# Last stage of a six-layer decoder: residuals and biases moved into TensorE's products, norms read from PSUM and ended on ScalarE

## The chip, the cores and the metric

The kernel runs on one core of one Trainium2 chip. The metric is the device time of one execution in microseconds. The kernel before takes 3324.82 us, the median of three runs (3321.77 to 3327.7).

## The reference, cut to what matters

Six residual layers follow one another, each ended by a layer norm without weights. The change touches the last stage of the kernel, which computes the last two layers on B = 2 sequences of S = 2048 tokens and D = 512 channels, all in float32:

```
x = layernorm(x + xattn(x, ctx))      # 16 heads of 32, 8 context rows per head (stride 16)
x = layernorm(x + tree(x))

xattn: Q = x Wq^T + bq; K, V from ctx with bk, bv
       out = softmax(Q K^T / sqrt(32)) V, then  @ Wo^T + bo
tree:  q = x Wq^T; gate = sigmoid(q routers^T)        # 255 inner nodes
       leaf_prob = product of the branch gates, depth 8 -> 256 leaves
       out = (leaf_prob @ leaf_values) @ Wout^T + Wout_b
layernorm(x) = (x - mean) / sqrt(var + 1e-5)
```

## The kernel before, in words

`decoder` calls five stages one after the other; a barrier lies between them. The last is `strided_attention_and_tree` (line 2361). It first loads all weights and multiplies them together once (`multiply_weights`, line 2503): the keys with Wq into `qk`, with the query bias as a row `qk_bias`; the values with Wo into `vo`; Wq of the tree with the routers into `wr`; the leaf values with Wout into `lo`. ScalarE copies each product out of PSUM (`keep_products`, line 2622).

Then it works through 16 tiles of 128 tokens of both sequences (b = 0 and 1). The work on one tile is spread over six steps of a software pipeline: step n handles tile n in its first part and tiles n-1 to n-5 in later ones. Each engine has its own `step(n)` (TensorE line 2598, ScalarE 2633, VectorE 2739, GpSimd 2483, the DMA queue SP 2458), executes it in the written order, and waits on counting semaphores. `pipelined` (line 44) writes the first six steps out, loops over pairs of steps, and writes the last ones out. Buffers with two places are chosen by `n.parity`.

The path of one tile, with the buffers that a later tile waits for:

- step n: `scores` (one-row product of the bias, four products with `xT`, for each b) into bank 0; VectorE `shift` (maximum per head, subtraction); ScalarE exp; VectorE `soften` (sum, reciprocal, product) into `probs`.
- step n+1: TensorE turns the probabilities (`turn_probabilities`, bank 1), ScalarE copies them, `attend` multiplies with `vo` into banks 2 and 3. VectorE `sum_attention` adds `x_bo`, which GpSimd has made of x and the bias; then statistics and aggregates (lines 168, 173), GpSimd's root of two operations (lines 189, 191), and `finish_attention` (line 184 by way of `Norm.finish`) writes `mid`.
- step n+2: `turn_mid` turns `mid` into bank 6, half by half (b), ScalarE copies each half (line 2646), `gates` multiplies with `wr` into bank 7, ScalarE tanh (line 2654) and an affine step (line 2657) make `gate`.
- step n+3: VectorE `walk_tree`, 16 dependent operations over 1 to 256 columns, two of them a level. GpSimd adds the output bias to `mid` into `mid_wb` (line 2490).
- step n+4: `turn_leaves` turns the leaf probabilities into bank 6, ScalarE copies them (line 2641), `feed` multiplies with `lo` into banks 4 and 5.
- step n+5: VectorE `sum_tree` adds `mid_wb`, statistics, GpSimd's root, `finish_tree` writes `o`; the next step stores it.

Bank 6 serves both `turn_mid` and `turn_leaves`. VectorE's step places the other operations between those of the tree by the index i of `walk_tree`; `soften` and `finish_attention` come behind it. TensorE's order in a step is: probabilities(n-1), leaves(n-4), scores(n), feed(n-4), mid(n-2) first half, attend(n-1), mid second half, gates(n-2) for both halves. With `Norm`, y is a tensor in SBUF, and PSUM is free again once VectorE has added; the sum's wait is in `sum_attention` and `sum_tree`.

Of the kernel before, what the change touches and what calls it, by code (L numbers as in the profile page):

```python
# [12 lines left out]
P = 128  # L13
F32 = mybir.dt.float32
BF16 = mybir.dt.bfloat16
ALU = mybir.AluOpType
# [9 lines left out]
class Tile:  # L26
# [8 lines left out]

    def slot(self):

        return slice(self.index, self.index + 1) if isinstance(self.index, int) else bass.ds(self.index, 1)
# [5 lines left out]
def pipelined(eng, steps, lag, step, more=1):  # L44

    first = lag + more + (steps - lag - more) % 2
    for n in range(first):
        step(Tile(n, n % 2, steps, n))  # L50
    with eng.Fori(0, (steps - first) // 2) as pair:
        step(Tile(pair * 2 + first, first % 2, steps, first))
        step(Tile(pair * 2 + (first + 1), (first + 1) % 2, steps, first + 1))
    for n in range(steps, steps + lag):
        step(Tile(n, n % 2, steps, n))
# [73 lines left out]
class Norm:  # L129
# [5 lines left out]
    def __init__(self, m, name, rows, summed=None):  # L135
        self.rows, self.summed = rows, summed
        self.y = m.sbuf(f"{name}_y", [P, rows, D])
# [49 lines left out]
    def root(self, pool, n, eps, exponent):  # L187
# [3 lines left out]
        pool.tensor_tensor(self.rstd[:], self.var_eps[:], exponent[:, 0:self.rows], ALU.pow).then_inc(self.rooted, 1)  # L191

# [1648 lines left out]


class ScaledNorm(Norm):


    def __init__(self, m, name, rows, summed=None):
        super().__init__(m, name, rows, summed)
        self.shift = m.sbuf(f"{name}_shift", [P, rows])
        self.finished = m.sem(f"{name}_finished")
        self.OPS = self.SUMMED + 2 * rows  # L1850
        self.ROOT_OPS = 4

    def root(self, pool, n, eps, exponent, zero):
        wait(pool, self.done, n, self.OPS, self.MOMENTS)
        wait(pool, self.finished, n, self.rows, 0)
        mean = self.moments[:, :, 0]
        pool.tensor_tensor(self.var_eps[:], self.moments[:, :, 1], eps[:, 0:self.rows], ALU.add).then_inc(self.rooted, 1)
        wait(pool, self.rooted, n, self.ROOT_OPS, 1)
        pool.tensor_tensor(self.rstd[:], self.var_eps[:], exponent[:, 0:self.rows], ALU.pow).then_inc(self.rooted, 1)
        wait(pool, self.rooted, n, self.ROOT_OPS, 2)  # L1860
        pool.tensor_tensor(self.shift[:], mean, self.rstd[:], ALU.mult).then_inc(self.rooted, 1)
        wait(pool, self.rooted, n, self.ROOT_OPS, 3)
        pool.tensor_tensor(self.shift[:], zero[:, 0:self.rows], self.shift[:], ALU.subtract).then_inc(self.rooted, 1)

    def finish(self, act, n, r, target):
        wait(act, self.rooted, n, self.ROOT_OPS, self.ROOT_OPS)
        act.activation(target, self.y[:, r], ACT.Identity, bias=self.shift[:, r:r + 1], scale=self.rstd[:, r:r + 1]).then_inc(self.finished, 1)

# [492 lines left out]
def strided_attention_and_tree(nc, x_in, xT_in, ctxT, weights, consts, out):  # L2361
# [8 lines left out]
    with ExitStack() as ctx:  # L2370
# [7 lines left out]
        bo_rep = sb("bo_rep", [P, D])  # L2378
        wb_rep = sb("wb_rep", [P, D])
# [6 lines left out]
        banks = [ps(f"bank{i}", [P, 512]) for i in range(8)]  # L2386
# [12 lines left out]
        CTX_LOADS, ATTENTION_LOADS, TREE_LOADS = 5, 3, 6  # L2399
# [4 lines left out]
        xb_sb = sb("x_bo", [P, 2, B, D])  # L2404
# [8 lines left out]
        mid = sb("mid", [P, 2, B, D])  # L2413
        midb = sb("mid_wb", [P, 2, B, D])
# [7 lines left out]
        norm_a, norm_f = Norm(m, "norm_a", B), Norm(m, "norm_f", B)  # L2422
# [4 lines left out]
        xb_done, midb_done = sem("xb_done"), sem("midb_done")  # L2427
# [6 lines left out]
        b_s, b_pT, b_o, b_f, b_T, b_g = banks[0], banks[1], banks[2:4], banks[4:6], banks[6], banks[7]  # L2434
# [4 lines left out]
        with nc.Block() as block:  # L2439
            @block.sync  # L2440
            def _(sp):
# [10 lines left out]
                sp.dma_start(ident[:], consts["ident"]).then_inc(attention_here, 16)  # L2452
                for to, k in ((mats["fq"], "fq"), (routersT, "routersT"), (leafT, "leafT"), (mats["outT"], "outT")):
                    sp.dma_start(to[:], block_rows(w[k])).then_inc(tree_here, 16)
                sp.dma_start(bo_rep[:], w["bo"].partition_broadcast(P)).then_inc(tree_here, 16)
                sp.dma_start(wb_rep[:], w["wb"].partition_broadcast(P)).then_inc(tree_here, 16)

                def step(n):
# [4 lines left out]
                    if t := n.back(LAG + 1):  # L2463
                        wait(sp, norm_f.done, t, norm_f.OPS, norm_f.OPS)
                        sp.dma_start(out_view[bass.ds(t.index * P, P)], o_sb[:, t.parity]).then_inc(stored[t.parity], 16)
                    if n:
                        wait(sp, xb_done, n, B, -B)
# [7 lines left out]
            def _(pool):  # L2475
                pool.memset(half[:], -0.5)
                pool.memset(eps[:], LN_EPS)
                pool.memset(center[:], 0.5).then_inc(ready, 1)
                pool.memset(ones[:], 1.0).then_inc(ready, 1)
                pool.memset(ones_row[:], 1.0).then_inc(ready, 1)  # L2480
                pool.wait_ge(tree_here, 16 * TREE_LOADS)

                def step(n):
                    if t := n.back(5):
                        norm_f.root(pool, t, eps, half)
                    if t := n.back(3):
                        wait(pool, norm_a.done, t, norm_a.OPS, norm_a.OPS)
                        wait(pool, norm_f.done, t, norm_f.OPS, norm_f.SUMMED - 2 * norm_f.OPS)
                        for b in range(B):
                            pool.tensor_tensor(midb[:, t.parity, b], mid[:, t.parity, b], wb_rep[:], ALU.add).then_inc(midb_done, 1)  # L2490
                    if n:
                        here(pool, x_here, n, 16)
# [352 lines left out]
```

## Time and profile before

| | |
|---|---|
| median of three runs | 3324.82 us |
| the profiled execution | 3335.67 us |
| its span, first to last instruction | 3333.9 us |
| mean granted TensorE clock | 0.894 |
| busy over the span: TensorE / VectorE / ScalarE / GpSimd | 81% / 75% / 35% / 19% |
| busy from 2975 to the end (359 us): TensorE / VectorE / ScalarE / GpSimd | 297.5 / 244.7 / 66.8 / 111.9 us |
| granted clock in that part | 0.86 |

The stages follow one another in time, so shares over the whole span say little of one of them. In the rows below, times are microseconds from the start of the span. PE is TensorE, DVE VectorE, ACT ScalarE, POOL GpSimd; L2564 is line 2564 of the kernel. A float32 product of 512 columns shows as two MATMUL rows, a transpose of 128 columns as one. Matmuls overlap each other in the rows, so what one costs is read from the distance between starts.

### The profile page before, as it was taken

What the parts mean: (1) busy time and instruction counts of PE and PEld (TensorE: products, weight loads), DVE (VectorE), ACT (ScalarE), POOL (GpSimd) and SP (SyncE); (2) the same over time, 40 slices, a digit from 0 to 9 for tenths busy, and PEclk for the clock granted to TensorE, in tenths of its full rate; (3) what the DMA queues carried; (4) which work ended last, traced back from release to release, by engine and by line L of the source; (5) the groups of instructions that cost most, each with busy time, mean ns of one, the idle gap of its engine ahead of it and who ended that gap; (6) DMA issues with size and microseconds to landing.
All of it is one profiled execution on the core that took longest, in us unless ns stands there. A gap on an engine that the chain in (4) does not pass through costs nothing. (4 is left out here: it accounts for less than half of the span.)

```text
span 3333.9 us, 88364 instructions
## 1 busy us (share of the span) xinstructions
PE 2692.8 (81%) x35334; PEld 1912.9 (57%) x35356; DVE 2510.2 (75%) x4464; ACT 1182.5 (35%) x2016; POOL 620.9 (19%) x800
## 2 busy tenths in 40 slices
PE   7577777777777755999999995697769999968987
PEld 5455655555555543677777763344456767646664
DVE  6888887888888872477777783887857787834887
ACT  5233333333333320122222221654446565521221
POOL 3232222333322221000000000002600000002343
PEclk9789888888888866999999997899989999988888
DMA  3000000010000101301111112545941212142231
GB/s 88 3 15 28 29 28 29 28 29 28 29 28 29 47 22 64 128 20 51 51 50 50 50 48 89 196 176 179 319 116 51 76 50 76 59 143 83 83 94 51
DMA packets 229643, 234.68 MB, mean 70 GB/s; under 512 B 24112, under 2 KB 157872, under 8 KB 229296
## 3 DMA queue, kind: packets, MB, share of 16 engines
q1 hardware_dynamic: 229296, 229.70, 21.6%
q8 instruction: 261, 4.28, 0.5%
q14 instruction: 86, 0.70, 0.1%
HBM read 136.84 MB, written 92.81 MB: 69 GB/s over the span
## 5 line engine op out<-in xcount | busy, mean ns | idle before, releaser
L1132 PE MATMUL ctxatt_banks<-ctxatt_xT,ctxatt_wq 128*128 128x256 f32 x1024 | 232.9, 381 | 2.9 <-ACT ctxatt_qT L1208 2.1
L1171 PE MATMUL ctxatt_banks<-ctxatt_wo,ctxatt_oT 128*128 128x512 f32 x512 | 230.8, 604 | 4.9 <-DVE ctxatt_norm_y L1277 4.9
L826 DVE TENSOR_TENSOR delta_a<-delta_t_sys 128x30 f32<-128x30 f32 (+14 forms) x480 | 223.3, 465 | 10.3
L849 DVE SCALAR_TENSOR_TENSOR delta_conv<-delta_line,delta_conv_w,delta_conv 128x256 f32<-128x256 f32 x384 | 206.9, 560 | 3.4 <-DVE delta_ss L772 2.1
L829 DVE TENSOR_TENSOR delta_t_sys<-delta_t_sys,delta_a 128x30 f32<-128x30 f32 (+14 forms) x480 | 200.2, 417 | 11.4
L1132 PEld LDWEIGHTS ctxatt_banks<-ctxatt_xT,ctxatt_wq 128*128 128x128 f32 x1024 | 190.0, 191 | 28.7 <-ACT ctxatt_qT L1208 3.3
L393 POOL TENSOR_TENSOR delta_conv<-delta_conv,delta_product 128x256 f32<-128x256 f32 x192 | 148.7, 784 | 263.0 <-ACT delta_product L658 262.7
L508 PE MATMUL delta_banks<-delta_states,delta_kqT 32*32 32x32 f32 x4096 | 60.3, 209 | 154.0 <-DVE delta_states L868 95.2
L489 PE MATMUL delta_banks<-delta_xT,delta_wkT 128*128 128x256 f32 x512 | 135.9, 416 | 43.3 <-ACT delta_beta_T L640 35.8
L656 ACT ACTIVATE delta_conv<-delta_line,delta_conv_b,delta_conv_w 128x256 f32<-128x256 f32 x192 | 115.3, 601 | 153.3 <-POOL delta_conv L393 141.6
L1171 PEld LDWEIGHTS ctxatt_banks<-ctxatt_wo,ctxatt_oT 128*128 128x128 f32 x512 | 96.4, 193 | 117.0 <-issue 110.5
L668 ACT ACTIVATE delta_u<-delta_banks 128x256 f32<-128x256 f32 x64 | 23.9, 373 | 385.6 <-PE delta_banks L508 385.6
L2080 PE MATMUL wkv_banks<-wkv_woT,wkv_oT 128*128 128x512 f32 x256 | 131.6, 673 | 36.0 <-DVE wkv_oT L2278 36.0
L489 PE MATMUL delta_banks<-delta_xT,delta_wqT 128*128 128x256 f32 x512 | 151.8, 450 | 0.0
L489 PE MATMUL delta_banks<-delta_xT,delta_wvT 128*128 128x256 f32 x512 | 143.9, 432 | 3.8 <-ACT delta_line L646 3.8
L508 PEld LDWEIGHTS delta_banks<-delta_states,delta_kqT 32*32 32x32 f32 x4096 | 52.5, 121 | 161.1 <-issue 161.0
L1218 ACT ACTIVATE ctxatt_probsT<-ctxatt_banks 128x512 f32<-128x512 f32 x128 | 69.4, 594 | 204.7 <-PE ctxatt_banks L1153 204.7
L2070 PE MATMUL wkv_banks<-wkv_mixed,wkv_wkT 128*128 128x256 f32 x512 | 118.0, 384 | 29.5 <-DMA wkv_wrT<-L_attn_wrT 29.5
L489 PEld LDWEIGHTS delta_banks<-delta_xT,delta_wkT 128*128 128x128 f32 x512 | 102.2, 206 | 64.6 <-issue 23.7
L499 PE MATMUL delta_banks<-delta_kqT 32*32 32x64 f32 x4096 | 91.3, 250 | 57.0 <-DVE delta_kqT L795 28.6
L189 POOL TENSOR_TENSOR ctxatt_norm_var_eps<-ctxatt_norm_moments,ctxatt_eps 128x2 f32<-128x2 f32 x16 | 3.1, 194 | 714.3 <-DVE ctxatt_norm_moments L173 714.3
L1271 DVE COPY ctxatt_oT<-ctxatt_banks 128x512 f32<-128x512 f32 x64 | 44.1, 690 | 119.3 <-PE ctxatt_banks L1163 119.3
(328 smaller groups left out, 6728.3 us busy)
## 6 DMA issues: line engine op xcount, KB each, us to landing
h<-ffn_hid SPq DMA_DIRECT2D x66, 256.0 KB, 2.0
ffn_hid<-h SPq DMA_DIRECT2D x6, 1536.0 KB, 13.0
wkv_xT<-xT SPq DMA_DIRECT2D x64, 129.0 KB, 2.8
delta_xT<-xT SPq DMA_DIRECT2D x64, 128.0 KB, 3.0
delta_x<-x SPq DMA_DIRECT2D x16, 512.0 KB, 3.6
xT<-delta_newT SPq DMA_DIRECT2D x64, 128.0 KB, 2.8
x<-delta_new SPq DMA_DIRECT2D x16, 512.0 KB, 3.5
ctxatt_xT<-xT SPq DMA_DIRECT2D x64, 128.0 KB, 2.6
```

The costliest lines, as they stand in the source:

```text
L393: pool.tensor_tensor(conv[:, i, g], conv[:, i, g], product[:, p % PRODUCTS], ALU.add).then_inc(tap_added, 1)
L489: mm = pe.matmul(b_proj[:, p % 2, 0:B * P], wT[NAMES[i]][:, k, g * P:(g + 1) * P], xT_sb[:, n.parity, k], start=k == 0, stop=k == KB - 1)
L499: mm = pe.matmul(cols[h, j], kqT[h, n.parity, 0, g * QI + j], kqT[h, n.parity, :, g * QI + j], start=True, stop=True)
L508: mm = pe.matmul(cols[h, lane], lhsT(h, lane), right(h, lane), start=True, stop=True)
L656: act.activation(conv[:, i, g].rearrange("p (b t) -> p b t", b=B), ln[:, :, 0:P], ACT.Identity, bias=conv_b[:, i, g:g + 1], scale=conv_w[: ...
L826: c.did(dve.tensor_tensor(terms, t_sys[:, j + 1:, j:j + 1].to_broadcast([P, rows, j]), t_sys[:, j:j + 1, 0:j].to_broadcast([P, rows, j]), ...
L829: c.did(dve.tensor_tensor(to, to, terms, ALU.add))
L849: c.did(dve.scalar_tensor_tensor(to, line[:, i, g, :, j:j + P], conv_w[:, i, g, j:j + 1], to, ALU.mult, ALU.add))
L1132: mm = pe.matmul(b_q[:, i * B * P:(i + 1) * B * P], wq[:, k, pair * P:(pair + 1) * P], xT_sb[:, n.parity, k], start=k == 0, stop=k == KB - 1)
L1171: mm = pe.matmul(b_o[:], oT[:, b, k, :], wo[:, k, :], start=k == 0, stop=k == PAIRS - 1)
L2070: mm = pe.matmul(bank(i, q)[:, j * WCOLS:(j + 1) * WCOLS], mats[name][:, k, u * P:(u + 1) * P], mixed[:, n.parity, i, k].rearrange("p b t ...
L2080: mm = pe.matmul(banks[:, OUT_BANK + r], oT[:, n.parity, k, r * P:(r + 1) * P], mats["woT"][:, k], start=k == 0, stop=k == KB - 1)
```

## The change

Both residual additions move to TensorE: a product with the identity matrix writes x (or the middle result) into the PSUM bank, and the product with the weights adds to it. The biases are added to `vo` (a sixteenth of it per head, since each head's probabilities sum to one) and to `lo` by a one-row product while the weights are multiplied. The norms read their input from PSUM, and the normalisation is an activation with scale and shift on ScalarE (`ScaledNorm`, which the stage before already used; its root has four operations on GpSimd in place of two). `x_bo`, `mid_wb` and GpSimd's additions are gone. `mid` has four places, chosen by `n.quarter`, and the loops of four engines are written over four steps (`pipelined_by_four`). The order within the steps of TensorE, ScalarE and VectorE is a new one. The DMA queue waits for `norm_f.finished` (ScalarE) and for `attended` (TensorE), and loads the biases as single rows.

```diff
@@ weights' products
-jobs.append((D, [(kv[1][:, e, b, :], mats["woT"][:, e, :]) for e in range(KB)]))
+jobs.append((D, [(kv[1][:, e, b, :], mats["woT"][:, e, :]) for e in range(KB)] + [(share_row[:], bo_row[:])]))
...
-jobs.append((D, [(leafT[:, e, l * P:(l + 1) * P], mats["outT"][:, e, :]) for e in range(KB)]))
+jobs.append((D, [(leafT[:, e, l * P:(l + 1) * P], mats["outT"][:, e, :]) for e in range(KB)] + [(ones_row[:], wb_row[:])]))
@@ TensorE
+                def start_attention(n):
+                    here(pe, x_here, n, 16)
+                    for b in range(B):
+                        wait(pe, norm_a.finished, n, B, b + 1 - B)
+                        pe.matmul(b_o[:, b], ident[:], x_sb[:, n.parity, b], start=True, stop=False)
 def attend(n):
     wait(pe, pT_kept, n, 1, 1)
     for b in range(B):
-        wait(pe, norm_a.done, n, norm_a.OPS, b + 1 - norm_a.OPS)
-        pe.matmul(b_o[b][:], pT_sb[...], vo[:, b, :], start=True, stop=True).then_inc(attended, 1)
+        pe.matmul(b_o[:, b], pT_sb[...], vo[:, b, :], start=False, stop=True).then_inc(attended, 1)
+                def start_tree(n):
+                    for b in range(B):
+                        wait(pe, norm_f.finished, n, B, b + 1 - B)
+                        pe.matmul(b_f[:, b], ident[:], mid[:, n.quarter, b], start=True, stop=False)
 def step(n):
-    turn_probabilities(t1); turn_leaves(t4, t3); scores(n); feed(t4)
-    turn_mid(t2, 0); attend(t1); turn_mid(t2, 1); gates(t2, 0); gates(t2, 1)
+    scores(n); start_attention(t1); turn_probabilities(t1)
+    start_tree(t4); turn_leaves(t4, t3); turn_mid(t2, 0); attend(t1)
+    turn_mid(t2, 1); gates(t2, 0); feed(t4); gates(t2, 1)
@@ ScalarE
+                def finish_attention(n, b):
+                    wait(act, midT_made, n, B, -B)
+                    wait(act, fed, n, B, -3 * B)
+                    norm_a.finish(act, n, b, mid[:, n.quarter, b])
+                def finish_tree(n, b):
+                    gone(act, stored, n, 16)
+                    norm_f.finish(act, n, b, o_sb[:, n.parity, b])
 def step(n):
-    probsT(t1); leafpT(t4); midT(t2, 0); midT(t2, 1); exps(n); gate_leaves(t2)
+    finish_tree(t5, 0); finish_tree(t5, 1); probsT(t1); leafpT(t4); midT(t2, 0)
+    exps(n); midT(t2, 1); gate_leaves(t2); finish_attention(t1, 0); finish_attention(t1, 1)
@@ VectorE, in the loop over the 16 tree operations i
-    walk_tree; sum_tree at 0, 1; norm_f.statistics at 2, 3; norm_f.aggregate at 4, 5; shift at 6, 7
-    finish_tree at 8, 9; sum_attention at 10, 11; norm_a.statistics at 12, 13; aggregate at 14, 15
-    behind the loop: soften(n); finish_attention(t1)
+    norm_f.statistics at 0, 1 and norm_f.aggregate at 2, 3, each ahead of walk_tree; shift at 4, 5
+    soften(n) at 11; norm_a.statistics at 12, 13; norm_a.aggregate at 14, 15
@@ GpSimd
-    norm_f.root(t5); mid_wb(t3); x_bo(n); norm_a.root(t1)
+    norm_f.root(t5); norm_a.root(t1)
```

The step functions are shown as the list of their calls; each part runs where its tile exists.

## Rows read from the trace of the kernel before

**Rows 1.** Timeline: start, duration in us, engine, line; [idle before <-releaser]
```profile
3032.24 0.48 PE L2555 MATMUL tree_bank<-tree_qk_bias,tree_ones_row 1*128 1x128 f32 x2 [0.69 <-ACT tree_lo L2630]
...
3094.40 0.60 ACT L2654 ACTIVATE tree_th<-tree_bank 128x512 f32<-128x512 f32 x1 [2.56 <-PE tree_bank L2564]
...
3191.90 0.60 ACT L2654 ACTIVATE tree_th<-tree_bank 128x512 f32<-128x512 f32 x1 [2.56 <-PE tree_bank L2564]
...
3226.30 0.60 ACT L2654 ACTIVATE tree_th<-tree_bank 128x512 f32<-128x512 f32 x1 [2.56 <-PE tree_bank L2564]
...
3260.90 0.60 ACT L2654 ACTIVATE tree_th<-tree_bank 128x512 f32<-128x512 f32 x1 [2.56 <-PE tree_bank L2564]
...
3276.82 0.60 ACT L2654 ACTIVATE tree_th<-tree_bank 128x512 f32<-128x512 f32 x1 [2.56 <-PE tree_bank L2564]
...
3328.97 1.00 DVE L184 TENSOR_SCALAR tree_o<-tree_norm_f_y,tree_norm_f_moments,tree_norm_f_rstd 128x512 f32<-128x512 f32 x2 [1.16 <-POOL tree_norm_f_rstd L191]
```

**Rows 2.** Timeline, TensorE's products of one step at full clock
```profile
3162.48 0.44 PE L2572 MATMUL tree_bank<-tree_ident,tree_probs 128*128 128x128 f32 x2 [0.59 <-DVE tree_probs L2699]
...
3162.75 0.60 PE L2587 MATMUL tree_bank<-tree_ident,tree_leaf 128*128 128x128 f32 x4
...
3163.28 0.48 PE L2555 MATMUL tree_bank<-tree_qk_bias,tree_ones_row 1*128 1x128 f32 x2
...
3166.19 3.60 PE L2595 MATMUL tree_bank<-tree_lo,tree_leafpT 128*128 128x512 f32 x8
...
3169.62 0.60 PE L2547 MATMUL tree_bank<-tree_ident,tree_mid 128*128 128x128 f32 x4
...
3170.06 1.88 PE L2579 MATMUL tree_bank<-tree_vo,tree_probsT 128*128 128x512 f32 x4
...
3172.22 3.62 PE L2564 MATMUL tree_bank<-tree_wr,tree_midT 128*128 128x256 f32 x16
```

**Rows 3.** VectorE by line: durations ns min/median/max; then groups, busy us, mean ns
```profile
L184 DVE TENSOR_SCALAR tree_o<-tree_norm_f_y,tree_norm_f_moments,tree_norm_f_rstd x32: 533/1406/1540, 3100.1 to 3329.4; 128x512 f32<-128x512 f32 x32
...
L2733 DVE TENSOR_TENSOR tree_norm_f_y<-tree_bank,tree_mid_wb 128x512 f32<-128x512 f32 x32 | 21.7, 686 | 3.0 <-PE tree_bank L2595 2.5
...
L168 DVE BATCH_NORM_STATS2 tree_norm_f_stats<-tree_norm_f_y 128x6 f32<-128x512 f32 x32 | 21.5, 686 | 0.0
```

**Rows 4.** Waits from 3099 to 3284: us in total, times, longest
```profile
PE tree_bank L2572 <- DVE tree_probs L2699: 19.8, 11, 2.9
```

**Rows 5.** Windows: us, PE, PEld, DVE, ACT, POOL busy, PEclk, DMA share, GB/s
```profile
3162.00:3164.00 2.00, 1.52 (x10) 1.24 (x11) 1.82 (x5) 1.89 (x4) 0.33 (x1) 1.00 0.00 0
...
3192.00:3194.00 2.00, 0.00 (x0) 0.00 (x0) 1.93 (x8) 1.22 (x2) 0.90 (x2) 1.00 1.01 321
...
3196.00:3198.00 2.00, 2.00 (x10) 1.77 (x9) 2.00 (x8) 0.04 (x1) 0.00 (x0) 0.50 0.00 0
```

**Rows 6.** Timeline, two groups of transposes into bank 6 with the copy between
```profile
3301.15 0.60 PE L2547 MATMUL tree_bank<-tree_ident,tree_mid 128*128 128x128 f32 x4
...
3302.50 0.66 PE L2547 MATMUL tree_bank<-tree_ident,tree_mid 128*128 128x128 f32 x4 [0.75 <-ACT tree_midT L2646]
```

**Rows 7.** Timeline, from the gates' products to the first tree operation
```profile
3289.90 3.62 PE L2564 MATMUL tree_bank<-tree_wr,tree_midT 128*128 128x256 f32 x16
...
3295.05 0.16 DVE L2727 TENSOR_TENSOR tree_paths<-tree_ones,tree_gate 128x2 f32<-128x2 f32 x1
```

**Rows 8.** Timeline, root and normalisation of ScaledNorm in the stage before
```profile
2963.70 0.20 POOL L1857 TENSOR_TENSOR wkv_norm_var_eps<-wkv_norm_moments,wkv_eps 128x2 f32<-128x2 f32 x1 [16.08 <-DVE wkv_norm_moments L173]
...
2965.36 1.52 ACT L1867 ACTIVATE wkv_new<-wkv_norm_y,wkv_norm_shift,wkv_norm_rstd 128x512 f32<-128x512 f32 x2 [2.98 <-POOL wkv_norm_shift L1863]
```

**Rows 9.** ScalarE by line: durations ns min/median/max
```profile
L2646 ACT ACTIVATE tree_midT<-tree_bank x32: 597/597/599, 3058.4 to 3303.2; 128x512 f32<-128x512 f32 x32
...
L2657 ACT ACTIVATE tree_gate<-tree_th,tree_center x16: 721/722/724, 3066.2 to 3307.3; 128x512 f32<-128x512 f32 x16
```

**Rows 10.** Timeline, the last feed of the drain
```profile
3319.32 6.14 PE L2595 MATMUL tree_bank<-tree_lo,tree_leafpT 128*128 128x512 f32 x8 [0.69 <-ACT tree_leafpT L2641]
```

More of the change, by code:

```diff
@@ L53, in pipelined, with pipelined_by_four @@
         step(Tile(pair * 2 + (first + 1), (first + 1) % 2, steps, first + 1))
+    for n in range(steps, steps + lag):
+        step(Tile(n, n % 2, steps, n))
+def pipelined_by_four(eng, steps, lag, step, more=1):
+    first = lag + more + (steps - lag - more) % 4
+    for n in range(first):
+        step(Tile(n, n % 2, steps, n))
+    with eng.Fori(0, (steps - first) // 4) as four:
+        for k in range(4):
+            step(Tile(four * 4 + (first + k), (first + k) % 2, steps, first + k))
     for n in range(steps, steps + lag):
@@ L1839, in _ @@
                     pipelined(pe, FSTEPS, 3, step)
[L1843 to L1867, printed above, removed]
 WT = P
@@ L2385, in strided_attention_and_tree @@
         ones_row = sb("ones_row", [1, P])
-        banks = [ps(f"bank{i}", [P, 512]) for i in range(8)]
+        share_row = sb("share_row", [1, P])
+        zero = sb("zero", [P, B])
+        all_banks = ps("banks", [P, 8, 512])
+        banks = [all_banks[:, i] for i in range(8)]
         mats = {k: sb(k, [P, KB, D]) for k in ("wkT", "wvT", "wq", "woT", "fq", "outT")}
@@ L2477, in _ @@
                 pool.memset(eps[:], LN_EPS)
+                pool.memset(zero[:], 0.0)
                 pool.memset(center[:], 0.5).then_inc(ready, 1)
                 pool.memset(ones[:], 1.0).then_inc(ready, 1)
-                pool.memset(ones_row[:], 1.0).then_inc(ready, 1)
-                pool.wait_ge(tree_here, 16 * TREE_LOADS)
+                pool.memset(ones_row[:], 1.0)
+                pool.memset(share_row[:], 1.0 / XH).then_inc(ready, 1)
                 def step(n):
                     if t := n.back(5):
[L2485 to L2492, printed above, removed]
-                        wait(pool, norm_a.done, n, norm_a.OPS, norm_a.SUMMED - 2 * norm_a.OPS)
-                        for b in range(B):
-                            pool.tensor_tensor(xb_sb[:, n.parity, b], x_sb[:, n.parity, b], bo_rep[:], ALU.add).then_inc(xb_done, 1)
+                        norm_f.root(pool, t, eps, half, zero)
                     if t := n.back(1):
-                        norm_a.root(pool, t, eps, half)
-                pipelined(pool, STEPS, LAG, step)
+                        norm_a.root(pool, t, eps, half, zero)
+                pipelined_by_four(pool, STEPS, LAG, step)
             @block.tensor
@@ new lines, in gate_leaves @@
+                def gate_leaves(n):
+                    wait(act, gated, n, B, B)
+                    wait(act, gate_done, n, 1, 0)
+                    act.activation(th[:], b_g[:], ACT.Tanh, scale=0.5).then_inc(th_done, 1)
+                    wait(act, th_done, n, 1, 1)
+                    wait(act, tree, n, TREE_OPS, 0)
+                    act.activation(gate[:].rearrange("p b n -> p (b n)"), th[:], ACT.Identity, bias=center[:], scale=0.5).then_inc(gate_done, 1)
+                def finish_attention(n, b):
+                    wait(act, midT_made, n, B, -B)
+                    wait(act, fed, n, B, -3 * B)
+                    norm_a.finish(act, n, b, mid[:, n.quarter, b])
@@ L2760, in step @@
                             norm_a.aggregate(dve, t1, b)
-                    if n:
-                        soften(n)
-                    for b in range(B):
-                        if t1:
-                            finish_attention(t1, b)
                 keep_keys_and_values()
-                pipelined(dve, STEPS, LAG, step)
+                pipelined_by_four(dve, STEPS, LAG, step)
 def decoder(nc, a, out):
```

173 lines of the change are left out of this document (93 added, 80 removed).

## The prediction

> **What bounds the kernel now.** The page gives 3333.9 us to this execution; the last stage begins near 2975 and all edits lie in it. Read first the timeline of ScalarE's tanh (line 2654), whose input is the last product of a step: it marks the end of each step. Step 4 ends at 3094.40 and step 15 at 3276.82, so the middle takes 182.4 / 11 = 16.58 us a step. Ahead lie 62.2 us from the first scores at 3032.24, behind it 57.1 us to the end of the span [rows 1].
>
> Next, TensorE's own rows of one step at full clock [rows 2]: probabilities turned 0.27, leaves turned 0.53, scores 2.91, feed 3.43 (four products of 512 columns, 0.86 each), half a middle result turned 0.44, attend 1.72 (two products), the other half 0.44, gates 3.44: 13.18 us, with 0.18 of drain behind. VectorE is the longer engine in such a step: one normalisation into tree_o takes 1.41 us by its median and 0.53 at its least, and each sum out of PSUM 0.69 [rows 3]. TensorE waits for VectorE's probabilities, 19.8 us in 11 waits [rows 4]. Where it waited over 2 us, its granted clock stood at 1.00 (2.4 GHz) in the gap and at 0.50 (1.2 GHz) 2 us behind it; where it was idle for 0.5 of 2 us, the clock stayed at 1.00 [rows 5]. The step from 3260.90 to 3276.82, 15.9 us, is one at full clock and VectorE's; the pair of steps that ends at 3226.30 holds a fall and took 34.4 [rows 1], 2.6 more than two such. So both engines are near the bound, VectorE at full clock and TensorE behind a fall.
>
> **VectorE and GpSimd: removed.** Per step four sums (4 x 0.69), the normalisations into tree_o (2 x 1.41) and those into tree_mid leave VectorE, over 6 us [rows 3]. GpSimd's four additions of 128x512 go with them. I price that at nothing in the middle: with over 6 us out of 15.9, VectorE is no longer last, and what is late next is TensorE.
>
> **TensorE: added.** Four identity products of 512 columns a step, two for x and two for the middle result. They have the form of the feed's products, so 4 x 0.86 = 3.44 us at full clock [rows 2]. The low bound is the rate of this kernel's transposes, four of 128 columns in 0.44 us, or 4 x 0.44 = 1.76. I take 3.44, since these are ordinary products. TensorE then has 16.62 us of work a step. In the weights' products four one-row products of 512 columns are added, all on an unbroken run: +3.4 us, low bound 1.8.
>
> **A wait inside the step.** The leaves are turned into bank 6 and, in the new order, the first half of the middle result follows directly into the same bank; before, scores and feed lay between. So TensorE waits for ScalarE's copy. The same pattern stands at the end of the trace: from one group of four transposes to the next, with the copy between, 1.35 us [rows 6]. In place of the 0.53 of rows 2 that is +0.82. This wait is sure.
>
> **A wait at the step's start.** PSUM banks now hold y until ScalarE has normalised it, and start_tree wants banks 4 and 5 in the same step in which the norm is read. Let T be the end of the gates. The first tree operation starts at T+1.53 [rows 7], and the second half's statistics are queued behind it on VectorE: they start at T+1.63, and the two aggregates among three tree operations end at T+2.8. GpSimd's root now has four operations; the stage before runs the same four, and from its first to ScalarE's start are 1.66 us [rows 8]. So ScalarE normalises from T+4.5. It took 0.76 a half there from SBUF. For PSUM I take off 0.125, the distance between a 128x512 activation out of SBUF (0.722) and out of PSUM (0.597) [rows 9], which gives 0.64; bounds 0.60 and 0.81. The first bank is free at T+5.2, the second at T+5.85. TensorE, after scores 2.91, identity products for x 1.72 and probabilities 0.27, is there at T+4.7 and waits 0.5 us. Queued behind it: leaves, middle, attend, gates, feed; on ScalarE the copies behind the normalisation. From T+5.21: 1.72 + 1.35 + 0.44 + 1.72 + 0.44 + 1.72 + 3.43 + 1.72 + 0.18 = 12.72, so the step takes **17.93 us**, 1.35 more than now. Bounds: 17.44 without this wait, 18.5 with root and activations at their longest.
>
> The Trainium skill, "VectorE: DVE Perf Modes", section on the TRN2 errata, gives VectorE 62 cycles of 0.96 GHz more for a PSUM source than for SBUF and ScalarE 52 cycles of 1.2 GHz less, 0.065 and 0.043 us. In the trace the sum out of PSUM (0.686) and the statistics out of SBUF (0.686) show no such step [rows 3], and ScalarE's distance is 0.125. By the page an estimate of the step would be 18.08, and the whole 1.6 us longer.
>
> **Other edits.** Scores come ahead of the probabilities; covered, since scores need only VectorE's shift. soften moves up to the eleventh tree operation, waits there for exps, which ScalarE does behind the first middle copy (T+10), and ends at T+11.4; the probabilities are wanted 11 us later. norm_a ends at T+14.4 on VectorE and 1.7 us later on GpSimd, ahead of ScalarE's turn at T'+1.4; its banks are free at T'+2.1 and T'+2.7 under scores of 2.91. If that cover went, it would cost up to 1.5 a step. SP's store waits for finish_tree (T+6.5) and so moves the next x and xT no nearer than 8 us to their use. Two broadcasts of bias rows become two row loads ahead of the wait at the weights: nothing, bound 1 us. Four buffers for mid and unrolling by four: nothing, bounds -1 and +3.
>
> **Fill.** From the first scores: step 1 ends at 11.4 (scores wait 1.3 for the shift, then 2.91, 1.72, 0.27, a 0.5 wait for the copy, 1.72). Step 2 ends at 24.0: scores, then 1.4 of waiting for norm_a's banks, then 1.72 + 0.27 + 0.44 + 1.72 + 0.44 + 3.44 with short copies. Step 3 ends at 35.0, step 4, the first with a tree, at 52.4. Now it is 62.2, with falls of the clock in it. Gain **-9.7**; bounds -13 and -4.
>
> **Drain.** Here the held bank costs most, since no scores cover it. At full clock steps 16 to 19 take 17.9, 17.1, 11.9 and 10.2, and the end another 8.1 (root 2.9, two halves 1.3, and 3.9 from there to the end of the span, as behind the last tree_o now [rows 1]): 65.2. TensorE stands idle for 2.4, 5.2, 5.2 and 3.6 us at their starts. After such gaps the last feed of now ran at the low clock, 6.14 in place of 3.43 [rows 10]; the four transposes ahead of the copy then take 0.45 more. So I add 2.5, 3.5, 4.7 and 4.4: 80.3 in all, against 57.1. **+23.2**; bounds +8 (full clock throughout) and +27.
>
> **Sum.** Weights +3.4, fill -9.7, middle 11 x 1.35 = +14.9, drain +23.2: +31.8 us on 3333.9, a span of 3366. The profiled execution took 3335.67 in all, 10.9 above the median of 3324.82; the difference is carried over: 3324.8 + 31.8 = **3357 us**.
>
> **The clock in the middle.** The new gaps are 0.5 and 0.8 us, far nearer to the short one of rows 5 than to the long, so I forecast 1.00 there.
>
> **Rivals.** (a) The forecast, chance 0.50. (b) The clock stays high in the drain as well: then +8.1 in place of +23.2, 3341 us, chance 0.22. For it: not each wait for VectorE was followed by a fall, as the step that ends at 3276.82 shows [rows 1]. Against it: the drain's feed of now [rows 10]. (c) The two short gaps together lower the clock in the middle in every second step; such a fall costs 2.6 us now, so +14: 3371 us, chance 0.11. Against it speaks the short gap of rows 5. (d) No change: the bank of norm_f is free before TensorE comes, 17.44 a step, the fill gains the full 13 and the drain stays at full clock with +6: 3.4 - 13 + 9.5 + 6 = +6, 3331 us, chance 0.10. (e) **Faster**: the identity products run at the transposes' rate. TensorE then has 14.9 us a step and 15.8 with the bank wait. If the tree's bank is free by T+3.1, the middle gives 11 x (15.8 - 16.6) = -9, weights +1.8, fill -13, drain +6: -14, 3311 us, chance 0.07. It decides from below 0.64 us a product. The rate of the transposes speaks for it; against it, feed and attend at 0.86 with the same types, and the chain over gate, statistics and root, which alone holds the step at 17.3. For the transposes the Trainium skill, "TensorE: Matmul & The Clock Gate", section Terms, names a transpose mode four times as fast for FP32; by that factor the estimate for four products would be 0.86 us, if they ran in it. The rows show the transposes twice as fast, 0.44 against 0.86 for 512 columns [rows 2].
>
> A measurement of this kernel tells about 0.2% from no change, 6.6 us. Slower by more: (a), (b), (c), 0.83. Within: (d), 0.10. Faster: 0.07. The range takes in (b) and most of (c): **3335 to 3380 us**.
>
> **What would show it.** Each identity product at 0.86 and TensorE's sum of 16.6 us a step; the first one into banks 4 and 5 waiting 0.5 us for ScalarE; 1.35 us from leaves to middle; the tanh every 17.9 us; VectorE idle for a third of the step; granted clock 1.00 in the middle and 0.50 in the drain. Wrong if identity products take under 0.6 us, if the statistics do not wait behind the first tree operation, or if the drain keeps its 57 us.

## The result, and the profile after

| | before | after |
|---|---|---|
| median | 3323.3 us (4 runs, 3318.6 to 3327.7) | 3367.4 us (4 runs, 3361.6 to 3373.9) |
| ratio, 95% interval | | 1.0133, 1.0109 to 1.0156 |
| span of the profiled execution | 3333.9 us | 3369.9 us |
| granted clock | 0.894 | 0.906 |
| TensorE / VectorE busy from 2975 to the end | 297.5 / 244.7 us | 340.4 / 133.2 us |

The change makes the kernel slower by 44 us. The forecast was 3357 us, range 3335 to 3380. All medians below are over every execution; one of e7's ten (3704 us) and one of e11's four (6209.5 us) were far slower than the rest, and without them the medians are 3337.0 and 3272.5.

The step marks answer to [rows 1]. Timeline of the changed kernel (start, duration in us, engine, line, [idle before <-releaser]), the first scores and six of the sixteen tanh:

```profile
3034.40 0.48 PE L2561 MATMUL tree_banks<-tree_qk_bias,tree_ones_row 1*128 1x128 f32 x2 [0.69 <-ACT tree_lo L2648]
...
3092.89 0.60 ACT L2675 ACTIVATE tree_th<-tree_banks 128x512 f32<-128x512 f32 x1 [6.29 <-PE tree_banks L2570]
3110.76 0.60 ACT L2675 ACTIVATE tree_th<-tree_banks 128x512 f32<-128x512 f32 x1 [6.29 <-PE tree_banks L2570]
...
3146.55 0.60 ACT L2675 ACTIVATE tree_th<-tree_banks 128x512 f32<-128x512 f32 x1 [6.29 <-PE tree_banks L2570]
3164.98 0.60 ACT L2675 ACTIVATE tree_th<-tree_banks 128x512 f32<-128x512 f32 x1 [6.29 <-PE tree_banks L2570]
3183.47 0.60 ACT L2675 ACTIVATE tree_th<-tree_banks 128x512 f32<-128x512 f32 x1 [6.29 <-PE tree_banks L2570]
...
3294.98 0.60 ACT L2675 ACTIVATE tree_th<-tree_banks 128x512 f32<-128x512 f32 x1 [6.29 <-PE tree_banks L2570]
```

Step 4 ends at 3092.89, step 15 at 3294.98: 202.1 / 11 = 18.37 us a step, against 16.58. The steps up to 3146.55 are written out and take 17.86 to 17.93; behind it the loop runs, with 18.43 to 18.77. The difference of the spans, 36.0 us, is the sum of four terms: start of the scores +2.2, fill (scores to step 4) 58.5 for 62.2 = -3.7, middle +19.7, drain 74.9 for 57.1 = +17.8.

One step's start, behind the tanh at T = 3110.76 (same view):

```profile
3112.14 0.16 DVE L2766 TENSOR_TENSOR tree_paths<-tree_ones,tree_gate 128x2 f32<-128x2 f32 x1 [4.13 <-ACT tree_gate L2678]
3112.22 0.69 DVE L183 BATCH_NORM_STATS2 tree_norm_f_stats<-tree_banks 128x6 f32<-128x512 f32 x1
...
3113.39 0.20 POOL L224 TENSOR_TENSOR tree_norm_f_var_eps<-tree_norm_f_moments,tree_eps 128x2 f32<-128x2 f32 x1 [5.33 <-DVE tree_norm_f_moments L188]
...
3114.95 1.45 ACT L234 ACTIVATE tree_o<-tree_banks,tree_norm_f_shift,tree_norm_f_rstd 128x512 f32<-128x512 f32 x2 [1.50 <-POOL tree_norm_f_shift L230]
...
3115.78 1.98 PE L2604 MATMUL tree_banks<-tree_mid,tree_ident 128*128 128x512 f32 x4
...
3117.60 0.60 PE L2598 MATMUL tree_banks<-tree_ident,tree_leaf 128*128 128x128 f32 x4
...
3118.89 0.66 PE L2553 MATMUL tree_banks<-tree_ident,tree_mid 128*128 128x128 f32 x4 [0.69 <-ACT tree_leafpT L2659]
```

The statistics stand behind the first tree operation, which waits for the gate; root and ScalarE follow, and TensorE's products into banks 4 and 5 (line 2604) start when the first half is normalised, at T+5.02. From leaves to middle 1.29 us pass for the copy. VectorE is idle for 4.13 us ahead of the step; from 3095 to 3300 it is busy for 43% of the time, while the granted clock is 1.00. The waits of TensorE from 3095 to 3300 (us in total, times, longest):

```profile
PE tree_banks L2553 <- ACT tree_leafpT L2659: 9.4, 11, 1.0
PE tree_banks L2604 <- ACT tree_o L234: 5.0, 9, 0.9
```

### The profile page after: what moved, and what is told of

Read it like the earlier page. It is cut to its first block and busy times, and to the rows that moved or that the text cites. A ratio compares the mean times of both kernels' runs of the same rounds, so it can differ in the third digit from the quotient of the medians.

```text
span 3369.9 us, 88338 instructions
## 1 busy us (share of the span) xinstructions
PE 2730.2 (81%) x35470; PEld 1917.0 (57%) x35492; DVE 2398.0 (71%) x4336; ACT 1228.1 (36%) x2080; POOL 549.8 (16%) x802
## 5 line engine op out<-in xcount | busy, mean ns | idle before, releaser
L869 DVE TENSOR_TENSOR delta_a<-delta_t_sys 128x30 f32<-128x30 f32 (+14 forms) x480 | 215.7, 449 | 10.3
L532 PEld LDWEIGHTS delta_banks<-delta_xT,delta_wkT 128*128 128x128 f32 x512 | 101.3, 204 | 64.5 <-issue 23.1
L591 PE MATMUL delta_banks<-delta_woT,delta_oT 128*128 128x512 f32 x256 | 128.0, 646 | 7.8 <-DVE delta_oT L935 6.9
L542 PE MATMUL delta_banks<-delta_kqT 32*32 32x64 f32 x4096 | 87.1, 241 | 58.2 <-issue 30.0
```

What stands on the lines that cost most here:

```text
L532: mm = pe.matmul(b_proj[:, p % 2, 0:B * P], wT[NAMES[i]][:, k, g * P:(g + 1) * P], xT_sb[:, n.parity, k], start=k == 0, stop=k == KB - 1)
L591: mm = pe.matmul(b_out, oT[:, g, b * P:(b + 1) * P], woT[:, g], start=g == 0, stop=g == KB - 1)
L869: c.did(dve.tensor_tensor(terms, t_sys[:, j + 1:, j:j + 1].to_broadcast([P, rows, j]), t_sys[:, j:j + 1, 0:j].to_broadcast([P, rows, j]), ...
```

## The experiments

T is the end of the gates, read as the start of the tanh. Fill runs from the first scores to step 4, drain from step 15 to the end of the span. "Middle" is the mean of the eleven steps from step 4 to step 15. Each kernel was timed beside the kernel before on the same chip; fill, middle and drain come from one profiled execution each.

| kernel | median us | ratio to before, 95% | fill | middle, a step | drain |
|---|---|---|---|---|---|
| before | 3323 | | 62.2 | 16.58 | 57.1 |
| after | 3367.4 | 1.0133 (1.0109 to 1.0156) | 58.5 | 18.37 | 74.9 |
| e1 no identity products | 3375.2 | 1.0138 (1.0117 to 1.0159) | 45.6 | 20.12 | 71.5 |
| e2 both waits covered | 3345.4 | 1.0056 (1.0036 to 1.0077) | 55.0 | 16.94 | 64.5 |
| e3 written out | 3361.7 | 1.0100 (1.0081 to 1.0119) | 58.5 | 17.91 | 72.8 |
| e9 one call moved | 3341.0 | 1.0058 (1.0037 to 1.0079) | 57.5 | 16.89 | 66.3 |
| e6 covered, no identity | 3298.6 | 0.9918 (0.9901 to 0.9934) | 54.6 | 13.83 | 59.4 |
| e4 biases only | 3290.9 | 0.9897 (0.9874 to 0.9921) | 58.5 | 13.97 | 47.8 |
| e7 e4 + spare additions | 3337.5 | 1.0037 (1.0024 to 1.0051) | 64.1 | 17.29 | 53.2 |
| e8 e4, scores first | 3290.1 | 0.9895 (0.9878 to 0.9911) | 50.1 | 14.48 | 46.5 |
| e5 sums on VectorE, norms end on ScalarE | 3274.7 | 0.9851 (0.9834 to 0.9867) | 58.2 | 13.14 | 42.5 |
| e10 e5, scores first | 3272.4 | 0.9853 (0.9833 to 0.9873) | 47.5 | 13.56 | 42.5 |
| e11 e5, both orders | 3274.9 | 0.9857 (0.9837 to 0.9877) | 54.2 | 13.14 | 42.5 |

**e1: the added work taken out, its waits kept.**

```diff
 wait(pe, norm_a.finished, n, B, b + 1 - B)
-pe.matmul(b_o[:, b], ident[:], x_sb[:, n.parity, b], start=True, stop=False)
 wait(pe, norm_f.finished, n, B, b + 1 - B)
-pe.matmul(b_f[:, b], ident[:], mid[:, n.quarter, b], start=True, stop=False)
```

> From the changed kernel, the four identity products of a step are left out, their waits stay; so x and the middle result are not added (the output lacks the residuals). It asks whether the step is as long as it is because TensorE has 3.44 us more to do. Theory A (the chain over the held banks is the bound): both banks of the tree are free only when ScalarE has normalised the second half, at T+5.8 (measured: first identity product starts at T+5.05, a half takes 0.76); from there leaves 1.35, middle 0.44, attend 1.72, middle 0.44, gate 1.72, feed 3.43, gate 1.72 and 0.18 make 11.0, so 16.8 us in written-out steps and 17.3 in the loop, against 17.9 and 18.4: 1.1 less in the middle, -12 us there and a few in the drain, about 3350 us. Rival T (TensorE's sum of work alone): 3.44 less in each of 19 steps, the step 14.9, about 3305 us.

The step did not get shorter, it got longer: 20.4 us in the loop. First TensorE's waits from 3099 to 3265, then windows of one step (us, busy PE, PEld, DVE, ACT, POOL, PEclk, DMA share, GB/s):

```profile
PE tree_banks L2597 <- ACT tree_o L234: 22.3, 8, 3.2
```

```profile
3223.00:3225.00 2.00, 1.81 (x12) 1.29 (x12) 1.89 (x10) 1.20 (x2) 0.46 (x2) 1.00 0.00 0
3225.00:3227.00 2.00, 0.00 (x0) 0.00 (x0) 1.60 (x9) 0.98 (x2) 0.83 (x3) 1.00 0.00 0
3227.00:3229.00 2.00, 1.11 (x4) 0.72 (x4) 0.00 (x0) 0.74 (x2) 0.00 (x0) 0.65 0.22 87
3229.00:3231.00 2.00, 1.11 (x5) 1.14 (x6) 0.00 (x0) 0.60 (x1) 0.00 (x0) 0.50 0.45 175
3231.00:3233.00 2.00, 2.00 (x3) 0.78 (x3) 0.98 (x3) 0.90 (x2) 0.00 (x0) 0.50 0.00 0
3233.00:3235.00 2.00, 2.00 (x8) 1.02 (x7) 1.79 (x5) 0.05 (x1) 0.00 (x0) 0.64 0.00 0
```

TensorE is through with scores and probabilities early and stands for 2.8 us before the held banks; behind this gap the granted clock is 0.50 for 6.8 us (worked out from the means of the windows). So rival T (the bound is TensorE's sum) is out: 3.44 us less work gave nothing. The kernel as a whole is not slower either: the ratios to the kernel before, 1.0138 and 1.0133, can't be told apart, since against the longer steps stand a fill that is 12.9 us and a drain that is 3.4 us shorter. My own 17.3 us for the loop was wrong too, since it left the clock out: 6.8 us at half speed cost 3.4, and the step is 3.1 longer. The clock fell behind gaps over 2 us before as well [rows 5]; I had taken the gap to be harmless in the one kernel that widens it.

**e2 and e9: the waits taken out, the work kept.** e2 has a new order on TensorE, and on ScalarE the tree's normalisation stands behind the two copies; e9 moves one call:

```diff
 if t4:
-    start_tree(t4)
     turn_leaves(t4, t3)
+    start_tree(t4)
```

> The changed kernel with another order on TensorE (leaves, attend, first half of the middle, then the identity products into banks 4 and 5 and feed, second half, gates) and ScalarE's finish_tree behind the two copies; all work stays. Both waits then lie beside other products. Theory A: the step is TensorE's 16.6 us of work plus 0.2, and up to 0.5 more in the loop: 17.1 in place of 18.37 in the middle, -14 us, and -4 to -10 in fill and drain: 3343 to 3350 us. Rival T: TensorE was idle in these waits, so it expects the same. Rival N (norms that read PSUM and end on ScalarE are slow in themselves): nothing changes in their number or kind, within 5 us of 3367.

> The changed kernel with one call moved: TensorE's identity products into banks 4 and 5 come behind the leaves' transposes and not ahead of them. The wait for the held banks then starts 0.53 us later, so the first is free in time, and the two products (1.72 us) lie over ScalarE's copy of the leaves, so the 0.82 us wait for bank 6 goes too. Theory A (two waits of together 1.3 us a step are what the changed kernel has above TensorE's 16.6 us of work): 16.8 to 16.9 a step written out and up to 17.3 in the loop, in place of 17.9 and 18.5; 3346 to 3356 us. Rival C (the chain gate, statistics behind the first tree operation, root, normalisation, then all products of the step sets the period, so that the wait only moves): T+5.2 and from there 1.72 + 0.44 + 1.72 + 0.44 + 1.72 + 3.43 + 1.72 + 0.18 = 11.4, 16.6 as well for the first bank; the second is free at T+5.85 in both. So the two differ only if ScalarE's copy of the leaves, which stands behind both normalisations, comes late: then bank 6 is free at T+7.1 and the step is 17.5, 3360 us.

e2 fell into theory A's range; e9 came 5 us below its own. Two written-out steps of e2, then of e9:

```profile
3091.55 0.60 ACT L2674 ACTIVATE tree_th<-tree_banks 128x512 f32<-128x512 f32 x1 [2.86 <-PE tree_banks L2570]
3108.43 0.60 ACT L2674 ACTIVATE tree_th<-tree_banks 128x512 f32<-128x512 f32 x1 [2.86 <-PE tree_banks L2570]
```

```profile
3086.09 0.60 ACT L2675 ACTIVATE tree_th<-tree_banks 128x512 f32<-128x512 f32 x1 [6.29 <-PE tree_banks L2570]
3102.67 0.60 ACT L2675 ACTIVATE tree_th<-tree_banks 128x512 f32<-128x512 f32 x1 [6.29 <-PE tree_banks L2570]
```

16.88 and 16.58 us: TensorE's sum of 16.62 from the prediction. From 3099 to 3240 no wait of TensorE for another engine shows in e2, and in e9 only two, 0.8 us together. e9's rival C named 16.6 for the first bank as well, so it is e2, with the banks long free, that speaks for TensorE's sum. In e9's loop the steps take 16.83 to 17.26, as the held banks are late again there. One moved call is worth 26 us of the 44, 8.6 of it in the drain. ScalarE's normalisation and the statistics out of PSUM are all still there, so they are not what costs these 26 us.

**e6: the identity products taken out once the waits are covered.** The edit is that of e1, on e2.

> The covered order of the changed kernel (leaves, attend, middle, then the tree's banks) with the four identity products left out, so without the residuals in the output. Left out of the changed kernel's own order they gave nothing: 20.4 us a step with TensorE waiting up to 3.2 us and the clock at 0.50 behind it. Theory A (chain first, TensorE's work second): with the waits covered TensorE's work is the bound, and its loss of 3.44 us shows in full: 16.96 goes to 13.5, or up to 14.2 where a wait for ScalarE is left; 3285 to 3300 us against 3345. Rival C (the identity products are cheap beside other products, or the clock falls again): 15.5 us a step or more, 3325 us or more.

13.6 us in the written-out steps 5 to 7 and 13.8 to 14.15 behind them, against 16.9: now 2.8 to 3.3 of the 3.44 us count. The same work was worth nothing behind the held banks and nearly its full price without them; there it costs 47 us in all (3345.4 against 3298.6).

**e3: no loop.** `pipelined_by_four` is replaced by `for n in range(steps + lag)` on four engines.

> The changed kernel with the last stage's steps of TensorE, VectorE, ScalarE and GpSimd written out in place of the loop by four; the queue SP keeps its loop. Theory A: the steps written out in the changed kernel took 17.87 to 17.93 us and those in the loop 18.43 to 18.77; with none in the loop all of the middle goes to 17.9, so 8 x 0.6 = -5 us: about 3362 us. Rival L (it is the position in the stage, data or DMA, not the loop): unchanged, within 2 us. Rival I (longer code has to be fetched): steps 8 to 15 longer than now, +5 us or more.

Two steps of e3 from the place where the changed kernel loops:

```profile
3180.59 0.60 ACT L2680 ACTIVATE tree_th<-tree_banks 128x512 f32<-128x512 f32 x1 [6.29 <-PE tree_banks L2575]
3198.51 0.60 ACT L2680 ACTIVATE tree_th<-tree_banks 128x512 f32<-128x512 f32 x1 [6.29 <-PE tree_banks L2575]
```

17.92 in every step: the 0.6 us a step were the loop's. Where TensorE does not wait the loop costs little: 16.96 against 16.88 in e2, 13.14 in both in e5. In the changed kernel's step behind the tanh at 3220.94, in the loop, the first tree operation starts at T+1.56 for 1.38 written out, GpSimd's root at 3.03 for 2.63, ScalarE at 4.58 for 4.19. What in the loop takes this time is left open.

**e4 and e7: the biases alone, and GpSimd's additions alone.** e4 is the kernel before with the biases in the weights' products, so that GpSimd adds nothing; e7 is e4 with four additions between spare buffers at the old place.

```diff
 e7, GpSimd's step
+for b in range(B):
+    wait(pool, spare_m, t, B, b)
+    pool.tensor_tensor(spare[:, 2], spare[:, 0], spare[:, 1], ALU.add).then_inc(spare_m, 1)
```

> The kernel before with one part of the change alone: the biases go into the weights' products, GpSimd's four additions of 128x512 a step and their buffers are gone, the middle result has four places and the loops go by four. Sums and norms stay on VectorE with 15.9 us a step before. Theory A: GpSimd's additions ran beside VectorE and stretched its operations; the normalisations into tree_o took 1.41 us by the median and 0.53 at the least, so 4 x 0.88 = 3.5 us go, VectorE's step is about 12.4, and TensorE with 13.18 and a wait for the probabilities is the bound: 13.6 to 15 us a step in place of 16.58, -17 to -33 us in the middle, +2 for the weights: 3290 to 3312 us, faster than both kernels. Rival V (the 1.41 us are the operation's own, whatever GpSimd does): step as before, 3322 to 3327 us.

> The kernel with the biases alone folded in (3290.9 us, 13.9 us a step) plus four additions of 128x512 a step on GpSimd at their old place, between buffers that nobody reads. No engine waits for them. If GpSimd's additions stretch VectorE's operations by being beside them (theory A), the normalisations into tree_o go from 0.54 back to 1.3 to 1.4 us and the step from 13.9 to 15.9 to 16.6, some of it as falls of the clock: 3318 to 3330 us. If the time went because VectorE and TensorE no longer wait for x_bo and mid_wb (rival W), the step stays at 13.9 and the time at 3291.

e4 is faster than both kernels, and time and step are in theory A's range. VectorE's normalisation by line, min/median/max in ns, answers to [rows 3]:

```profile
L199 DVE TENSOR_SCALAR tree_o<-tree_norm_f_y,tree_norm_f_moments,tree_norm_f_rstd x32: 539/545/547, 3091.0 to 3282.3; 128x512 f32<-128x512 f32 x32
```

And the timeline of e7, where nobody waits for the additions, and from 3085 to 3290 VectorE is never seen to wait for GpSimd's roots:

```profile
3118.83 2.67 POOL L2509 TENSOR_TENSOR tree_spare<-tree_spare 128x512 f32<-128x512 f32 x2
3118.89 1.48 DVE L199 TENSOR_SCALAR tree_o<-tree_norm_f_y,tree_norm_f_moments,tree_norm_f_rstd 128x512 f32<-128x512 f32 x1
3121.46 2.67 POOL L2515 TENSOR_TENSOR tree_spare<-tree_spare 128x512 f32<-128x512 f32 x2
3121.47 1.53 DVE L199 TENSOR_SCALAR tree_o<-tree_norm_f_y,tree_norm_f_moments,tree_norm_f_rstd 128x512 f32<-128x512 f32 x1
```

One addition and the normalisation by line, in e7 (min/median/max in ns):

```profile
L2509 POOL TENSOR_TENSOR tree_spare<-tree_spare x32: 1260/1266/1332, 3068.4 to 3321.7; 128x512 f32<-128x512 f32 x32
L199 DVE TENSOR_SCALAR tree_o<-tree_norm_f_y,tree_norm_f_moments,tree_norm_f_rstd x32: 533/548/1542, 3103.4 to 3336.3; 128x512 f32<-128x512 f32 x32
```

Each of the two normalisations starts with one of GpSimd's additions (1.26 us) and ends 0.28 us behind it: VectorE is held until the addition is over. The kernel before shows the same, and the small tree operation between the two normalisations takes 1.26 us, where an undisturbed one of its size takes 0.18 to 0.19:

```profile
3100.08 2.67 POOL L2490 TENSOR_TENSOR tree_mid_wb<-tree_mid,tree_wb_rep 128x512 f32<-128x512 f32 x2
3100.14 1.49 DVE L184 TENSOR_SCALAR tree_o<-tree_norm_f_y,tree_norm_f_moments,tree_norm_f_rstd 128x512 f32<-128x512 f32 x1
3101.55 1.26 DVE L2725 TENSOR_TENSOR tree_paths<-tree_paths 128x32 f32<-128x32 f32 x1
```

The Trainium skill, "SBUF — State Buffer", section "SBUF: two separate sides", calls the port pair of the two engines an exclusive lock: of a GpSimd operation and a VectorE operation that needs the pair (in a two-port mode, or with two sources in SBUF), whoever starts first holds it for its whole instruction. These rows agree. In the records of the kernel before, the eleven tree operations of 128x32 that start inside an addition end 0.05 us behind it, and held normalisations some 0.28 behind; the maximum over the scores, which reads PSUM, keeps its 0.42 beside an addition. The operations that started inside an addition took 53 us more in all than their like outside, 3.3 a step, and 48 us more in e7. The median of the normalisation did not go back to 1.3 to 1.4 as expected: in e7 more of the holding falls on tree operations.

e7's step is back at 17.29, clock falls included (0.88 granted from 3099 to 3240, against 1.00 in e4), and it is 0.4% slower than the kernel before and 8 us above theory A's range; why it overshoots is open. Rival W (the waits for GpSimd's results) is out, since e7 has none.

**e8: a miss.** TensorE's order is leaves, scores, probabilities.

> The kernel with the biases alone folded in, with TensorE's order changed in one place: leaves, scores, probabilities in place of probabilities, leaves, scores. There TensorE waited 0.5 us a step for VectorE's probabilities; now scores cover it. Theory A: the step is TensorE's 13.18 us of products and 0.15 of drain, 13.3 to 13.5 in place of 13.9: -6 to -9 us, 3282 to 3286 us. Rival V (VectorE is the bound with its sums behind attend and soften at the end, and only passes the wait on): 13.7 to 13.9, 3288 to 3292 us.

The step grew to 14.4 to 14.7. In the timeline, TensorE's feed in place of the wait for the probabilities:

```profile
3170.90 0.38 ACT L2640 ACTIVATE tree_probsT<-tree_bank 128x256 f32<-128x256 f32 x1 [2.30 <-PE tree_bank L2575]
3171.18 0.59 ACT L2644 ACTIVATE tree_leafpT<-tree_bank 128x512 f32<-128x512 f32 x1
...
3171.82 3.70 PE L2598 MATMUL tree_bank<-tree_lo,tree_leafpT 128*128 128x512 f32 x8 [1.04 <-ACT tree_leafpT L2644]
```

ScalarE copies the probabilities ahead of the leaves, so later probabilities make the leaves late: a wait of 0.5 us was traded for one of 1.0. I had looked at TensorE's order alone. The fill is 8.4 us shorter and the middle 5.7 longer; the medians are alike.

**e5, e10, e11: what beats both.** e5 keeps the biases and ScalarE's normalisation of the changed kernel, but VectorE adds the residuals, so that PSUM is free at once. The orders on VectorE and ScalarE are new as well, and the diff names TensorE's alone:

```diff
-norm_a, norm_f = ScaledNorm(m, "norm_a", B, attended, b_o), ScaledNorm(m, "norm_f", B, fed, b_f)
+norm_a, norm_f = ScaledNorm(m, "norm_a", B), ScaledNorm(m, "norm_f", B)
...
+dve.tensor_tensor(norm_a.y[:, b], b_o[:, b], x_sb[:, n.parity, b], ALU.add).then_inc(norm_a.done, 1)
...
 TensorE: probabilities, scores, leaves, attend, mid 0, feed, mid 1, gates
```

> From the changed kernel: the biases stay in the weights' products and the norms still end on ScalarE, but the residuals are added by VectorE from PSUM into SBUF, so that no identity product and no held bank is left; TensorE's order is probabilities, scores, leaves, attend, first middle half, feed, second half, gates. Theory A (held banks and identity products are what the change costs, ScalarE's normalisation in itself costs nothing): TensorE's 13.2 us of products are the bound, 13.3 to 13.9 us a step, 3280 to 3292 us. Rival N (ScalarE's normalisation lies on the chain and lengthens it by its 1.45 us against VectorE's 1.0 and by the root's two more operations): the step is 14.5 or more, 3297 us or more, slower than the kernel with the biases alone (3290.9).

Window of e5 from 3099 to 3240 (columns as above):

```profile
3099.00:3240.00 141.00, 139.86 (x651) 97.05 (x651) 111.03 (x357) 69.57 (x118) 27.82 (x86) 1.00 0.33 105
```

TensorE is busy for 99% of it at full clock, 13.14 us a step, its own 13.18 of products [rows 2]. Step and time lie below theory A's range. 3274.7 us is 1.5% under the kernel before and 2.8% under the changed one.

> The fastest kernel so far (biases folded, sums on VectorE, norms ended on ScalarE; 3274.7 us) with scores ahead of the probabilities on TensorE. In its middle TensorE has no wait, 13.14 us a step; so nothing changes there. In its first steps TensorE waits 2.94 and 3.46 us for the probabilities, and the granted clock is 0.50 for 20 of the first 27 us. Theory A (gaps of about 3 us bring the low clock): with scores over them the gaps shrink and most of the fill runs at full clock, from first scores to the second tanh 26 to 30 us in place of 35.6: 3265 to 3270 us. Rival D (the low clock comes anyway, since VectorE's chain from scores to probabilities is as long): within 2 us of 3274.7. Rival E (as with the kernel of the biases alone, the copies behind the later probabilities become late and the step grows): 13.6 or more a step, 3281 us or more.

> The kernel with sums on VectorE and norms ended on ScalarE, with scores ahead of the probabilities in the steps 0 to 3 only, and the probabilities first from step 4 on. Measured apart: with scores first everywhere the second tanh comes 24.5 us behind the first scores and not 35.6, since the granted clock stays at 1.00 (it was 0.50 for most of 27 us behind waits of 2.9 and 3.5 us for the probabilities); with the probabilities first the step is 13.14 us and not 13.6. Theory A (the two effects are apart and add): 24.5 in the fill and 13.14 in the middle, 3263 to 3268 us. Rival D (the fall of the clock at the start comes and goes with something else than these waits): 3270 to 3276 us.

e10's fill ran at full clock and was 10.7 us shorter; its step grew to 13.6, as rival E had it, though its time did not; TensorE waits 0.2 us a step before attend for the probabilities' copy. e11 has the step of e5 and, with the same first steps as e10, still found the clock at 0.50 from its first scores: 54.2 in place of 47.5. So e10's fast fill need not come from its order; e11's time lies in rival D's range. The medians of the three can't be told apart. That the orders add in the fill is not shown.

## Why the prediction was right in direction and short by 10 us

- **The step.** Forecast 17.93, measured 17.86 to 17.93 where it is written out. First product into the held banks at T+5.02 (forecast 5.2), leaves to middle 1.29 (1.35). That it fits to 0.1 us is in part luck, since its parts were off and cancelled: ScalarE starts at T+4.19 and not 4.5, and takes 0.76 to 0.77 a half and not 0.64, and the two products into the held banks take 1.82 and not 1.72. The 0.125 that I took off for PSUM came from two different activations. The same activation in the stage before, out of SBUF, takes 0.81 and not the 0.76 that I read as half of a pair; so PSUM saves 0.03 to 0.04, close to the 0.043 that the prediction cites. VectorE's statistics take 0.01 more out of PSUM (0.699 for 0.686), far below the 0.065 cited. The activation in the changed kernel, out of SBUF and out of PSUM (min/median/max in ns):

```profile
L234 ACT ACTIVATE wkv_new<-wkv_norm_y,wkv_norm_shift,wkv_norm_rstd x32: 798/807/816, 2496.6 to 2962.5; 128x512 f32<-128x512 f32 x32
...
L234 ACT ACTIVATE tree_o<-tree_banks,tree_norm_f_shift,tree_norm_f_rstd x32: 769/774/778, 3097.1 to 3365.0; 128x512 f32<-128x512 f32 x32
```

- **A mis-sized term: the loop.** "Four buffers for mid and unrolling by four: nothing, bounds -1 and +3." The middle took 19.7 - 14.9 = 4.8 us more than forecast, and none of it in the written-out steps. e3 shows it: without the loop 17.91 a step, and 5.7 us less in the median, which by itself would lie within the spread of the changed kernel's runs. The loop's cost stands where a chain of waits sets the step (here) and hardly where TensorE does (e2, e5); that each wait in a loop is what costs is an argument and not shown.
- **TensorE's sum.** 16.62 was right (e9: 16.58), and that the chain stands above it too. What the text did not say is how lopsided it is: e1 shows that taking the added work out gains nothing in this order, e9 that the place of one call decides.
- **Removed work priced at nothing.** Right for this change, since VectorE was no longer last; it is idle for 57% of the middle, where a third was forecast. That 15.9 us is VectorE's step rests on two of the eleven steps; in the kernel before most go in pairs, 13.95 and 18.9 to 20.7. And the 1.41 us of a normalisation [rows 3] were taken as VectorE's load; they were GpSimd's additions holding it up, and the part of the change that removed them is worth 32 us by itself (e4, 3290.9). The rest of the change took that and 44 us more.
- **Fill.** Forecast -9.7, measured -3.7. Step 3 came as worked out (11.3 for 11.0), step 4 too (17.5 for 17.4); the two before were 5.7 too long together, since the clock was at 0.50 from the first scores on, behind a gap of only 0.69 us. e2 issues the same instructions there, the same gap ahead, and ran at 1.00: 25.4 us to its first tanh, against 29.7. First e2, then the changed kernel:

```profile
3036.97 1.16 PE L2563 MATMUL tree_banks<-tree_qk,tree_xT 128*128 128x128 f32 x8
```

```profile
3036.86 2.08 PE L2563 MATMUL tree_banks<-tree_qk,tree_xT 128*128 128x128 f32 x8
```

  At the low clock the second scores and the products of x took 5.3 and 3.4 us (between starts) for 2.9 and 1.7: 4 of the 6 us. Why the clock fell is open, so in every fill of the table some us are chance: it was low there in the changed kernel, e3, e6, e9 and e11, and full in e1, e2 and e10.
- **Drain.** Forecast +23.2, measured +17.8: the waits at the starts of the last three steps came as forecast (5.20, 5.20 and 3.59 us), but less was lost to the low clock behind them. Behind the first gap of 5.20 us the clock was low for 3.4 us and back at 1.00, which costs 1.7 us where I had put 3.5. Steps 16 and 17 took 18.9 each, for 20.4 and 20.6, and the rest 37.1 for 39.3.
- **Weights.** +2.2 for +3.4; but the first scores lie between 3026.1 and 3036.6 in kernels with the same weights' code, so this term is below what one profile can show.
- **Rivals.** (b) and (c) did not come: the middle kept 1.00, the drain did not. (d) is out with the 44 us. (e) is out: e6 prices an identity product at 0.70 to 0.83 us, above the 0.64 from which it would decide. The 10 us between forecast and median are 4.2 of spans (36.0 for 31.8) and 6.6 of the profiled execution of before, which stood 10.9 above its median while that of after stands 4.3 above. The 4.2 are a sum of larger errors, weights -1.2, fill +6.0, middle +4.8 and drain -5.4; that they nearly cancel is luck.

## What to carry to other kernels

Adding a residual inside PSUM saves VectorE a pass, but it makes the bank's next use wait for the whole norm behind it; count from where the bank comes free, not only the products. Put other work of the engine between such a wait and what is late: here one moved call gave 26 us. And when an operation's median is 2.6 times its minimum, ask first which engine runs beside it, since that may be worth more than moving the operation.

## What the runs showed of the hardware

- Less work on TensorE made the step longer (e1: 20.1 us for 18.4) and the kernel no faster, by way of a gap of 2.8 us and the low clock behind it.
- One GpSimd addition of 128x512 between SBUF tensors (1.3 us) holds up VectorE operations between SBUF tensors that start beside it until it ends: a normalisation of 128x512 takes 1.5 for 0.54, a tree operation of 128x32 1.26 for 0.19. The maximum over the scores out of PSUM keeps 0.42 beside it. Sums and statistics take 0.69, but none of them stood beside an addition.
- The same first instructions ran at 1.00 in e2 and at 0.50 in the changed kernel; TensorE's rows before them are alike.
